# One 512-column product for each group of four scaled rows, waits carried by the instruction behind them, and a ring of sixteen scaled rows

## What is computed

```python
items_emb = item_table[items]
user_emb = user_table[users]
hist_emb = user_table[history_users]
scores = jnp.einsum('bhd,bd->bh', hist_emb, user_emb)
user_his_emb = jnp.einsum('bh,bhd->bd', scores, hist_emb)
x = jnp.concatenate([items_emb, user_his_emb, user_emb], axis=1)
x = _dice(_batchnorm(x @ W1 + b1, g1, be1), a1)
x = _dice(_batchnorm(x @ W2 + b2, g2, be2), a2)
return x @ W3 + b3
```

## Time and profile before

| | us |
|---|---|
| median of 3 runs | 1003.19 |
| lowest, highest | 1000.81, 1003.52 |
| profiled execution | 1003.54 |
| its span, first to last instruction | 1001.5 |
| gathers, first to last | 30.5 to 812.7 |

### The profile page before, as it was taken

How to read it: one execution, slowest core, us unless ns; L and a number is a source line. 1 busy time by engine, 2 the same in 40 slices (tenths; PEclk the granted TensorE clock), 3 DMA queues, 4 the chain that set the end, 5 groups by cost and what they waited for, 6 DMA issues and landing times.

```text
span 1001.5 us, 16389 instructions
## 1 busy us (share of the span) xinstructions
PE 655.3 (65%) x3743; PEld 611.8 (61%) x3743; DVE 520.6 (52%) x1339; ACT 338.9 (34%) x879; POOL 490.8 (49%) x580
## 2 busy tenths in 40 slices
PE   4464655647474747466567465756766469999998
PEld 3463655547473736456467455755665469888888
DVE  7553444344453526354436354644344526999748
ACT  3111222223132313132223132332223237778546
POOL 6646544454555454636454635545544534281025
PEclk8776675757675666766676677858676679999999
DMA  7112111111111111111111111111111110000000
GB/s 218 38 35 44 35 34 35 35 42 33 42 36 39 30 45 26 44 27 42 32 38 33 45 25 42 35 34 39 40 34 33 43 22 1 2 0 1 1 1 2
DMA packets 17236, 34.61 MB, mean 35 GB/s; under 512 B 8104, under 2 KB 8400, under 8 KB 17168
## 3 DMA queue, kind: packets, MB, share of 16 engines
q0 software_dynamic: 14208, 29.13, 11.8%
q1 hardware_dynamic: 2960, 4.67, 1.4%
HBM read 33.76 MB, written 0.01 MB: 34 GB/s over the span
## 4 chain that ended last, share of the span: by engine, by line
PE 44%; another core or an unknown queue 26%; issue 15%; ACT 6%; DVE 4%; ACTq 4%; DVEq 1%; PEld 0%; PEldq 0%
PE ps L1489 14%; PE ps L1549 10%; PE ps L1409 7%; ACT scaled L1244 4%; PE ps L1425 3%; ACTq L1244 2%; PE ps L1475 2%; PE ps L1499 1%; PE ps L1564 1%; PE ps L1388 1%; ACT h L1230 1%; PE ps L1633 1%; PE ps L1430 1%; ACTq L1265 1%
## 5 line engine op out<-in xcount | busy, mean ns | idle before, releaser
L520 POOL DMA_INDIRECT rows<-in_L_rec_user_table_dram,slot_idx x432 | 411.6, 953 | 378.9 <-ACT scaled L1244 252.3
L1489 PE MATMUL ps<-ident,scaled 128*128 128x128 f32 x982 | 211.5, 384 | 228.1 <-ACT scaled L1244 188.0
L1489 PEld LDWEIGHTS ps<-ident,scaled 128*128 128x128 f32 x982 | 188.8, 285 | 245.6 <-issue 237.1
L1244 ACT ACTIVATE scaled<-rows,work 128x128 f32 (+1 forms) x491 | 157.3, 392 | 256.6 <-remote 162.0
L834 DVE TENSOR_TENSOR prod<-rows,ps 128x512 f32<-128x512 f32 x122 | 83.7, 686 | 152.9 <-issue 79.4
L711 DVE SCALAR_TENSOR_TENSOR h<-ps,col_no 128x1024 f32<-128x1024 f32 (+1 forms) x34 | 39.2, 1161 | 164.4 <-ACT ranked L1211 75.6
L1549 PE MATMUL ps<-h,w 128*128 128x256 f32 (+1 forms) x576 | 113.3, 356 | 1.0 <-DVE h L1064 1.0
L1409 PEld LDWEIGHTS ps<-wide,h 128*128 128x128 f32 x512 | 100.3, 297 | 16.9 <-issue 16.9
L1409 PE MATMUL ps<-wide,h 128*128 128x104 f32 x512 | 102.5, 382 | 9.7 <-issue 9.7
L1549 PEld LDWEIGHTS ps<-h,w 128*128 128x128 f32 x576 | 99.6, 190 | 12.8 <-issue 1.2
L840 DVE TENSOR_REDUCE work<-prod 128x512 f32 (+1 forms) x122 | 83.7, 686 | 35.3 <-issue 20.4
(11 more groups left out here) (219 smaller groups left out, 806.4 us busy)
## 6 DMA issues: line engine op xcount, KB each, us to landing
rows<-in_L_rec_user_table_dram,slot_idx POOLq DMA_INDIRECT x432
w<-in_L_rec_W_dram SPq DMA_DIRECT2D x1, 2048.0 KB
w<-in_L_rec_W_dram SPq DMA_DIRECT2D x1, 1536.0 KB
h<-in_r_history_users_dram SPq DMA_DIRECT2D x2, 400.0 KB, 3.5
wide<-in_L_rec_user_table_dram,own_idx POOLq DMA_INDIRECT x5
wide<-in_L_rec_item_table_dram,own_idx POOLq DMA_INDIRECT x5
last_row<-in_L_rec_user_table_dram SPq DMA_DIRECT2D x1, 64.0 KB
last_item<-in_L_rec_item_table_dram SPq DMA_DIRECT2D x1, 64.0 KB
```

What stands on the lines that cost most here:

```text
L520: nc.gpsimd.indirect_dma_start(rows[:, s, :], None, user_table, bass.IndirectOffsetOnAxis(slot_idx[:, s:s + 1], 0)).then_inc(landed[s], 16)
L1244: nc.scalar.activation(scaled[:, j, :], rows[:, bass.ds((g & (GROUPS - 1)) * GROUP + j, 1), :], ACT.Copy, scale=score[:, bass.ds(g * GROUP ...
L1489: mm = nc.tensor.matmul(pooled_ps, scaled[:, j, :], ident[:, :], start=False, stop=False, skip_group_check=True)
```

## The change

1. `scaled` becomes a ring of sixteen rows. ACT may scale group g when PE has summed group g - 4 (`pair_summed` starts at 4 in place of 1). The end group goes to a buffer of its own, `end_rows`; in the last tile all groups do, and there ACT waits for the group just before, as it did.
2. PE adds a group by one product: the identity is the weights, and the four rows, 512 columns, are the moving side. The sum is then not transposed and stands in four quarters of a PSUM bank. It waits once for a group, not four times. The last tile keeps four products of 128 columns.
3. At a tile's end ACT copies the 512 columns (`quarters`). PE adds and transposes the four quarters by four more products in the next tile, ahead of the two transposes of the own rows, and ACT's `both_T` has 384 columns in place of 256. Layer 1 of the pooled row waits for that copy.
4. PE takes `g0` before the last row, not after it. ACT scales a fourth group ahead of its loop.
5. `hold` no longer raises `passed`, so that the wait is carried by the next instruction on the engine, often one that computes a register. `hold_apart` keeps the old form at four places (POOL's `rows_free`, DVE's `keys_cut` and `sorted_out`, and the rare loop over own rows).

```diff
-        scaled = sb("scaled", [P, GROUP, D])
+        scaled = sb("scaled", [P, RING * D])
+        end_rows = sb("end_rows", [P, GROUP, D])
+        quarters = sb("quarters", [P, GROUP, D])
...
         def hold(eng, semaphore, value):
+            if not isinstance(value, int) or value > 0:
+                eng.wait_ge(semaphore, value)
+
+        def hold_apart(eng, semaphore, value):
+            hold(eng, semaphore, value)
             if not isinstance(value, int):
-                eng.wait_ge(semaphore, value)
                 eng.sem_inc(passed, 1)
-            elif value > 0:
-                eng.wait_ge(semaphore, value)
...
+            def scale_rows(g, t):
+                if not isinstance(g, int):
+                    g = act.snap(g).with_bounds(max_val=HIST * (t + 1) // GROUP - 1)
+                hold(act, scored, g + (t + 1))
...
+                hold(act, pair_summed, g + (GROUPS if t == TILES - 1 else 1))
...
+                for j in range(GROUP):
+                    to = end_rows[:, j, :] if t == TILES - 1 else scaled[:, bass.ds(at + j * D, D)]
+                    sc = nc.scalar.activation(to, rows_flat[:, bass.ds(at + j * D, D)], ACT.Copy,
+                                              scale=score[:, bass.ds(pair + j, 1)])
+                sc.then_inc(rows_free, 1)
...
-                nc.scalar.activation(pooled_T[:, :], pooled_ps, ACT.Copy).then_inc(pooled_kept, 1)
+                if t < TILES - 1:
+                    nc.scalar.activation(quarters[:, :, :], quarter_ps, ACT.Copy).then_inc(pooled_kept, 1)
...
-            pe.sem_inc(pair_summed, 1)
+            pe.sem_inc(pair_summed, GROUPS)
...
+            def add_rows(g, t, first=False):
...
+                hold(pe, rows_free, g + 1)
...
+                    mm = nc.tensor.matmul(ps[:, 1, :], ident[:, :], scaled[:, bass.ds(at, GROUP * D)], start=first, stop=False,
                                           skip_group_check=True)
                 mm.then_inc(pair_summed, 1)
...
                 if t:
                     pe.wait_ge(both_kept, t)
+                    for q in range(GROUP):
+                        nc.tensor.matmul(turn_ps[:, 2 * P:3 * P], quarters[:, q, :], ident[:, :], start=(q == 0), stop=(q == GROUP - 1),
+                                         skip_group_check=True)
```

More of the change, by code:

```diff
@@ L181, in recommender_kernel @@
         last_scaled = sb("last_scaled", [P, D])
-        both_T = sb("both_T", [P, 2 * P])
+        both_T = sb("both_T", [P, 3 * P])
         pooled_T = sb("pooled_T", [P, P])
@@ L1231, in keep_layer1 @@
                                          bias=b1c[:, m:m + 1]).then_inc(l1_kept, 1)
-            def scale_rows(g, t, after):
-                by_slot = t == TILES - 1 and after is end_scaled
-                count = GROUP - 1 if by_slot else GROUP
-                if not by_slot:
+            rows_flat = rows.rearrange("p s d -> p (s d)")
+            def scale_rows(g, t):
[3 more added lines that the diff above has]
+                hold(act, pair_summed, g + (GROUPS if t == TILES - 1 else 1))
+                at = (g & (GROUPS - 1)) * (GROUP * D)
+                pair = g * GROUP + t * GROUP
+                if not isinstance(g, int):
+                    at, pair = act.snap(at), act.snap(pair)
+                for j in range(GROUP):
[3 more added lines that the diff above has]
+                sc.then_inc(rows_free, 1)
@@ L1237, in scale_rows, with scale_end @@
+            def scale_end(g, t):
+                last = t == TILES - 1
+                g = act.snap(g).with_bounds(max_val=HIST * (t + 1) // GROUP - 1)
+                if last:
+                    hold(act, pair_summed, g + GROUPS)
+                else:
                     hold(act, scored, g + (t + 1))
-                for j in range(count):
-                    if by_slot:
+                at, pair = act.snap((g & (GROUPS - 1)) * (GROUP * D)), act.snap(g * GROUP + t * GROUP)
+                for j in range(sum(n for _, n in END_PARTS) if last else GROUP):
+                    if last:
@@ L1240, in scale_rows @@
                         act.wait_ge(end_scored, END_PARTS.index(max(part for part in END_PARTS if part[0] <= j)) + 1)
-                    if j == 0:
-                        hold(act, pair_summed, g + (t + 1))
-                    nc.scalar.activation(scaled[:, j, :], rows[:, bass.ds((g & (GROUPS - 1)) * GROUP + j, 1), :], ACT.Copy,
-                                         scale=score[:, bass.ds(g * GROUP + (t * GROUP + j), 1)]).then_inc(
-                                             slot_scaled if j < GROUP - 1 else after, 1)
+                    sc = nc.scalar.activation(end_rows[:, j, :], rows_flat[:, bass.ds(at + j * D, D)], ACT.Copy,
+                                              scale=score[:, bass.ds(pair + j, 1)])
@@ L1248, in _ @@
+                    if last or j == GROUP - 1:
+                        sc.then_inc(slot_scaled if last else end_scaled, 1)
             for t in range(TILES):
@@ L1255, in _ @@
                                      scale=last_weight[:, 0:1]).then_inc(last_ready, 1)
-                for i in range(3):
-                    scale_rows(g0 + i, t, rows_free)
+                for i in range(GROUPS):
+                    scale_rows(g0 + i, t)
                     if i == 0:
                         act.wait_ge(turned, t + 1)
-                        nc.scalar.activation(both_T[:, :], turn_ps, ACT.Copy).then_inc(both_kept, 1)
-                    elif t:
+                        n = 3 * P if t else 2 * P
+                        nc.scalar.activation(both_T[:, 0:n], turn_ps[:, 0:n], ACT.Copy).then_inc(both_kept, 1)
+                    elif t and i < 3:
                         keep_layer1(t - 1, 4 * i - 4)
@@ L1264, in _ @@
                         keep_rows(1)
-                with act.Fori(g0 + 3, g1) as g:
-                    scale_rows(g, t, rows_free)
+                with act.Fori(g0 + GROUPS, g1) as g:
+                    scale_rows(g, t)
                 if t + 2 < TILES:
                     keep_rows(t + 2)
-                scale_rows(g1, t, end_scaled)
+                scale_end(g1, t)
                 if t == 0:
@@ L1531, in _ @@
                     keep_busy(3)
[L1532 to L1534 removed]
+                add_end(t)
             keep_busy(1)
```

74 lines of the change are left out of this document (46 added, 28 removed).

## The result

The changed kernel takes **976.04 us** (median of 5 runs, 972.77 to 978.41) where the kernel before takes 1003.19: a ratio of 0.9731, 95% interval 0.9703 to 0.9759. It is faster by 27 us, where 61 were forecast. The profiled execution is one of 977.62 us.

The account below looks back on a forecast made before the run. POOL's gathers set the floor, 540 us, but some 240 us are lost waiting because ACT frees rows late. 1003.5 - 61 - 10 + 30 - 20 = 942 us; range 880 to 1015 (0.81).

Parts of the forecast that it names:

- The ring: ACT's scaling in the loop: no wait for PE's last sum, POOL saves 4.1 us once a tile, 61 us.
- the second rival: POOL's wait only moves, standstills last longer after longer streaks; ring gives 15 us; 998 us in all, chance 0.17.
- fewer instructions: PE's loop, DVE's sorting rounds, ACT: fewer instructions shorten waits before `ranked` and layer 1's copies, 20 us, bounds 0 to 65.
- Cheaper waits: Waits carried by the next instruction, 366 for 122 groups, mostly hidden on DVE: 10 us saved, bounds 0 and 37.
- The 512-column product: PE's one product a group lengthens the tile boundary: 2.0 us a tile, 30 us added, bounds 0 and 59.
- standstills: Loop and boundary: ACT resumes 6.8 or 7.6 us late, about 3 us after the start of POOL's last gather.
- the pile: Instructions issued beside the gathers, candidate cause of standstills; fewer should shorten the waits, 20 us, bounds 0 to 65.
- "Remote" before the scaling under 50: Sign for the ring: ACT's waits marked "remote" before its scaling fall from 162 us to under 50.
- The boundary from 6.3 to about 7.5: Sign at the tile boundary: from `ranked` to POOL's next gather, 6.3 us becomes about 7.5.
- Waits of 4 to 5 us in the loop gone: Sign for the ring: POOL's loop waits of 4 to 5 us vanish, with streaks of 12 gathers and more.
- Waits before `ranked` of 6 to 8 us: Sign for the pile: ACT's waits before `ranked` average 6 to 8 us in place of 9.2.
- The rule weighed: Fetches at taken branches: by the skill's rule standstills stay where they are, since every loop and branch is kept.

Follow-up runs that it names:

- the moved placement: Against the changed kernel, second half of the key placement moved ahead of the loops: 967.5 us with standstills, 756.9 without.

## Why the prediction was wrong, and what of it held

**The ring** (forecast 61 us, measured 7) is the term that failed. ACT was to scale at about 349.6, and POOL was to go straight on and save 4.1 us once in a tile. The first part came true: there is no "remote" wait before the scaling, streaks of 16 and 20 gathers are common where 8 and 12 stood, and POOL's waits of 3 us and more away from the boundary are 14 in place of 33. The step that failed is to count each such wait as saved, as if the other engines kept their pace in the time gained. They crawl while POOL gathers, so the 29 us that the ring takes out of the loops come back at the boundaries, 29 us. The prediction named that as its low end, "if POOL only runs into the next wait", and as the second rival's mechanism, priced there at 15 us, and the result lies in its span of 970 to 1003. I had the row for it, a longer streak followed by a longer wait, and weighed it at 0.17.

The terms add up: the ring gave 54 us less than forecast, the product and the fewer instructions together 21 more (below), the carried waits 1 less, which makes the 34 us between 942 and 976. That the result is no further off is the luck of two errors of opposite sign.

**Cheaper waits** (10, measured 9 alone). The gap between DVE's dependent steps fell from 0.28 to 0.18 us, as asked for. Right, though beside the ring the part is worth anything from 0 to 8.

**The 512-column product** (+30) and **fewer instructions** (-20) can't be measured apart with standstills. Together, from the run with carried waits to the one without the ring, they give 11 us (993.0 to 981.9, on one occasion), where the forecast had them cost 10; in the table they take 21 us out of the loops and put 12 at the boundaries. With the gathers replaced, where neither standstill nor crawl is seen, the whole change costs 17 to 19 us net of the cheaper waits, which is near 30 - 10. If the boundary costs the same with standstills, the pile is worth some 30 to 40 us; that is worked out, not shown. What is shown is its size for another edit: 306 products more on PE cost 50 us with standstills and nothing with the gathers replaced. The pile stood in the forecast with 20, bounds 0 to 65; by this it was right in kind and too small. The product itself takes 2.07 us at the boundary, where I worked out 1.73 from the rows of layer 2, and the boundary is longer by 3.2 us, of which 2 are hidden, between my 1.1 and 3.9.

**The checks.** "Remote" before the scaling under 50: right, it is none. The boundary from 6.3 to about 7.5: 7.0. Waits of 4 to 5 us in the loop gone: wrong, about one in a tile is left. Waits before `ranked` of 6 to 8 us: wrong, 181.0 in 16 is 11.3. POOL's waits for ACT's `scaled` fell below the 120 at which I had called the forecast wrong, to 97.5, but mostly because other releasers took them over; I had asked for one releaser where the sum over all, 378.9 to 359.2, was what counts.

**The pile itself** was half understood. The runs showed that gathers are needed (724.9 us and 4 slow register instructions with them replaced) and that more instructions beside them cost more; they showed too that both together are not enough, since in the other condition the same kernel has no slow one. I had taken a standstill to be of a given length, to be avoided or shortened. It ends, as the crawl does, when POOL's streak has ended.

**The rule weighed.** The page holds 26 packets of kind instruction in its DMA table for the moved placement both with standstills and without, and the loops and branches are the same, at 967.5 and 756.9 us. In the trace these packets take 1.13 us each with standstills and 1.11 without, so a fetch under way is no slower; how long one waits before its packet starts isn't recorded. The rule that the prediction weighed from the Trainium skill ("Runtime: NRT & Kernel Launch", Instruction fetch mechanics), that a taken branch to a page outside the two held forces a fetch before execution goes on, therefore doesn't tell the two apart by itself. Nor did the standstills stay where they were, as the prediction had it by that rule: before layer 1's copies the "remote" waits fell from 115.0 to 16.8 us with every loop kept.

## What to carry over

Before pricing a freed wait at its full length, ask what the other engines do in the time gained: where they are slowed for as long as the freed engine runs, it is given back at the next place where all meet. Sum a bottleneck's waits over all its releasers, "issue" included, before reading a change in one. And where a slow-down may belong to the condition of a chip, run the kernel before and the changed one with the suspected traffic replaced by on-chip work of about the same pace: here it turned a gain of 27 us into a cost of 17 to 19.

## What I had not expected of the hardware

- One kernel takes 1001.5 or 746.8 us on a chip of one number, at other times. The changed kernel with its gathers replaced takes 724.9 and 724.2 in the two conditions: the difference is all in what runs beside the gathers. The cause of the condition stays open.
- Beside indirect gathers at 1.25 us each, with standstills, the other engines slow at times: PE to one weight load in 1.4 to 2.9 us, ACT and DVE to register instructions of 0.7 us on average (166 us for 234, 7 of them on POOL) where 0.05 is the median.
- In that condition 306 float32 products more, which are 612 records and as many weight loads, cost 50 us, 0.16 us a product, though PE is busy for 62% of the span; with the gathers replaced they cost nothing (722.8 beside 724.2).
- Half a row, or half of the rows, in each gather makes nothing faster there: 952.7 and 966.4 us beside 953.3, with as many packets.
- A float32 product of 512 columns shows as two records and 2.07 us at the boundary, with a mean of 0.776 us a record in the loop.
